# Alignment distances handed to the wavefront in two parts, and context rows loaded in their own order

## The chip, the cores and the metric

The kernel runs on one core of a Trainium2 chip. The metric is the time of one launch in microseconds (us). Five engines take part, each with its own instruction stream: TensorE (PE) for matmuls and transposes, VectorE (DVE), ScalarE (ACT), GpSimd (POOL), and SyncE (SP), which issues most DMAs. ACT and POOL issue DMAs as well. They meet only through semaphores: an instruction `wait_ge` stops the whole stream of the engine on which it stands.

## The reference, cut to what matters

Four blocks follow each other on `x` of 4 batches x 512 tokens x 128 channels, with a context of 4 x 77 keys x 128 channels. Only the first one is touched by the change:

```python
x = x + tanh(g_xattn[0]) * align(ctx_1024, layernorm(x))     # changed block
x = x + tanh(g_ffn[0])   * moe_64_experts(layernorm(x))
x = x + tanh(g_xattn[1]) * attention(layernorm(x), ctx_1024)
x = x + tanh(g_ffn[1])   * moe_8_experts(layernorm(x))

def align(small, large):                  # 77 keys, 512 tokens, per batch
    D = sqrt(max(aa[:, None] + bb[None] - 2 * small @ large.T, 0))
    R[i, j] = D[i, j] + min(R[i-1, j], R[i, j-1], R[i-1, j-1])
    walk back from (76, 511) to (0, 0) along the smallest neighbour
    expanded[j] += small[i]  for every cell (i, j) of that path
```

## The kernel before, in words

**Distances.** The recurrence over 77 x 512 cells is run from both ends at once: direction d = 0 takes the upper keys 0 to 38 (`HALF` = 39 rows, on partitions 0 to 38), direction d = 1 the lower keys in reverse order (`LOWER` = 38 rows, on partitions 64 to 101) with the tokens reversed too. `ctx_sb` holds the context in this order. The upper half is loaded by SP; the lower half is first copied row by row in reverse order into a scratch in device memory (`scr_ctx`, issued by ACT), then loaded from there by ACT. PE transposes `ctx_sb` (line 1056), ACT writes `ctxT_neg` and `ctxT` (lines 806, 809), DVE makes the squared sums `aa` (`context()`, lines 1508 and 1510). For each batch, the token rows are normalised on DVE and POOL, transposed on PE (`turn`), squared on ACT, and multiplied with `ctxT_neg` (`distances`, lines 1089 to 1093). ACT takes the root (`dist_root`, lines 840 to 844, with `aa` as the bias), DVE corrects it (`corrected`, lines 1522 to 1528) and counts `s_dist` up, once per batch.

**Lanes.** The recurrence runs as a wavefront. Tokens are cut into 15 chunks of 35 columns; chunk c of batch b is one partition (a lane), and at step s lane c handles row s - c. So a row of `d2` on one partition has to be spread over 15 partitions, each one slot later. This goes through the scratch `scr_d`: `store_dist` (line 457) writes 39 rows x 15 chunks of 140 bytes, `load_lanes` (line 464) reads 15 lanes of 53 slots (`SLOTS`) into `dl`. There are 8 stores and 8 loads (4 batches x 2 directions), all on SP but two loads that ACT issues. `scr_d` is zeroed beforehand (line 551, counted by `s_zero`).

**Forward steps.** DVE waits for all eight loads (`lanes_laid`) and then does 53 steps (lines 1571 to 1582). From step 38 on, each step has cells at which the two directions meet.

**Beside it.** PE, ACT, SP and POOL prepare 25 groups of second-MoE weights: SP loads a group (`load_prep`, lines 495 and 499, two buffers; the load of group g waits until PE has transposed group g - 2), PE transposes it (line 1131), ACT copies it (line 926), POOL stores it. On SP's queue the loads of groups 2 and up stand behind the last `load_lanes`. PE does parts of the value projection (lines 1109, 1110) after each of the first 12 groups, and the products that find the meeting column (`meet(c)`, lines 1117 and 1119) after groups 9, 10, 11 and 12, four per group (three after the last). DVE's `meeting()` (line 1610) waits for all fifteen.

**Backward steps.** 53 steps on DVE (lines 1628 to 1632) with the path cells made in pieces of four slots (`cells`, line 1605). Path cells go back to a row layout through `scr_on`, in three parts (`ON_PARTS` = slots 25 to 52, 5 to 24, 0 to 4): `store_path` (line 474) waits for the pieces of that part, and `load_path` (line 483, four DMAs, one per batch) for the store. SP does this for d = 0, ACT for d = 1. When all rows are there, PE makes the aligned sum (line 1153), and the next block begins.

Of the kernel before, what the change touches and what calls it, by code (L numbers as in the profile page):

```python
# [21 lines left out]
F32 = mybir.dt.float32  # L22
# [7 lines left out]
P = 128  # L30
# [6 lines left out]
def program(nc, x, ctx_1024, g_xattn, g_ffn, r0_w, sg0, su0, sd0, eg0, eu0, ed0,  # L37
# [14 lines left out]
    COLS = CH * CW  # L52
# [3 lines left out]
    DROWS = [slice(0, HALF), slice(64, 64 + HALF)]  # L56
    KROWS = 64 + HALF
# [3 lines left out]
    LSLOT = 64 + SLOTS  # L61
    LANE = LSLOT * CW
    ON_LANE = SLOTS * CW
    assert 2 * HALF - KEYS in (0, 1) and HALF <= 64 and 16 * B == 64
# [55 lines left out]
    with ctx:  # L120
# [13 lines left out]
        scr_ctx = nc.dram_tensor("scr_ctx", (B, LOWER, H), F32).ap()  # L134
# [29 lines left out]
        aa = sb("aa", [KROWS, B])  # L164
        aasq = sb("aasq", [KROWS, B, H])
# [6 lines left out]
        lane_table = sb("lane_table", [P, TABLE])  # L172
# [91 lines left out]
        ON_PARTS = [(25, SLOTS), (5, 25), (0, 5)]  # L264
# [94 lines left out]
        s_crev = sem("ctx_reversed")  # L359
# [30 lines left out]
        s_dst = [sem(f"dist_stored{b}") for b in range(B)]  # L390
        s_dld = sem("dist_lanes")
        s_upper = sem("wave_upper")
# [61 lines left out]
        def store_dist(engine, d, b):  # L454

            first = DROWS[d].start
            engine.dma_start(at(scr_d[b], first * CW, [[CW, HALF], [LANE + CW, CH], [1, CW]]),
                             d2[DROWS[d], b, :].rearrange("i (c w) -> i c w", w=CW)).then_inc(s_dst[b], 16)

        def load_lanes(engine, d, b):  # L460

            engine.wait_ge(s_dst[b], 32)
            first = FIRST_SLOT[d]
            engine.dma_start(dl[lanes(d, b)].rearrange("c s w -> c (s w)"),
                             scr_d[b, :, first:first + SLOTS].rearrange("c s w -> c (s w)")).then_inc(s_dld, 16)
# [4 lines left out]
        def store_path(engine, part, d):  # L470

            first, last = ON_PARTS[part]
            engine.wait_ge(s_on, 2 * ON_PIECES[part])
            engine.dma_start(scr_on[d, :, :, first:last, :].rearrange("b c s w -> (b c) (s w)"),
                             on[64 * d:64 * (d + 1), first:last].rearrange("c s w -> c (s w)")).then_inc(s_onst[d], 16)

        def load_path(engine, part, d):

            first, last = ON_PARTS[part][0], (HALF, LOWER)[d] if part == 0 else ON_PARTS[part][1]
            engine.wait_ge(s_onst[d], 16 * (part + 1))  # L480
            for b in range(B):
                cells = pmask[64 * d + first:64 * d + last, b, PAD * (1 - d):PAD * (1 - d) + COLS].rearrange("i (c w) -> i c w", w=CW)
                engine.dma_start(cells if d == 0 else cells[:, ::-1, :],
                                 at(scr_on[d, b], first * CW,
                                    [[CW, last - first], [ON_LANE + CW, CH], [1, CW]])).then_inc(s_path[d], 16)
# [20 lines left out]
        POOL_CONST = 25  # L506
# [143 lines left out]
        def _(pool):  # L650
            for p0 in (32, 96):
                nc.gpsimd.memset(ctx_sb[p0:p0 + 32], 0.0).then_inc(s_cz, 1)
            pool.wait_ge(s_cz, 2)
# [47 lines left out]
            pool.wait_ge(s_pool, 20)  # L701
            lane_constants(slice(0, 16), 0, 0)
            pool.wait_ge(s_pool, 24)
# [98 lines left out]
        def _(act):  # L802
            def context():
                act.wait_ge(s_ct, 1)
                turned = ps[6].rearrange("p (b r) -> p b r", b=B)
                nc.scalar.activation(ctxT_neg[:], turned, ACT.Copy, scale=-2.0).then_inc(s_ctn, 1)
                for first, rows in ((0, slice(0, HALF)), (HALF, slice(64, 64 + LOWER))):
                    n = rows.stop - rows.start
                    nc.scalar.activation(ctxT[:, :, first:first + n], turned[:, :, rows], ACT.Copy).then_inc(s_ctn, 1)

            def lane_tables():

                act.wait_ge(s_lt, 1)
                nc.scalar.activation(lane_table[:], ps[7][:, 0:TABLE], ACT.Copy).then_inc(s_lc, 1)
                nc.scalar.activation(rst[:, 0, 0:1], ps[7][:, CORNER:CORNER + 1], ACT.Copy).then_inc(s_lane, 1)
# [21 lines left out]
            def dist_root(b):  # L837

                act.wait_ge(s_ab, b + 1)
                nc.scalar.activation(d2[0:KROWS, b, 0:S], dist_bank(b)[0:KROWS], ACT.Relu, bias=aa[:, b:b + 1]).then_inc(s_d2, 1)  # L840
# [11 lines left out]
            def norm(k):  # L852
                for b in range(B):
                    root(k, b)
                    if k == 0 and b == 0:
                        context()
                    if b >= 1:
                        high(k, b - 1)
                    if k == 0 and b == 1:
                        lane_tables()  # L860
                    if k == 2 and b >= 2:
                        query(b - 2)
                if k == 0:
                    act.wait_ge(s_aa, 1)
# [11 lines left out]
            act.wait_ge(s_cz, 2)  # L876
            act.wait_ge(s_crev, 16)
            act.dma_start(ctx_sb[64:64 + LOWER], scr_ctx.rearrange("b k d -> k b d")).then_inc(s_ctx, 16)
# [13 lines left out]
            for b in (2, 3):  # L892
                load_lanes(act, 1, b)
# [28 lines left out]
            for g in range(GROUPS[1]):  # L922
# [129 lines left out]
        def _(pe):  # L1052
# [5 lines left out]
            pe.wait_ge(s_pool, 24)  # L1058
            nc.tensor.matmul(ps[7][:, 0:TABLE], repeat_lane[:], by_lane[:], start=True, stop=True).then_inc(s_lt, 1)

            def turn(k, b):
# [10 lines left out]
                mm.then_inc(s_xt, 1)  # L1072

# [8 lines left out]
            def distances(b):  # L1082
# [5 lines left out]
                top, bottom = dist_bank(b)[0:64, :], dist_bank(b)[DROWS[1], :]  # L1088
                nc.tensor.matmul(top, ctxT_neg[:, b, 0:64], xT0[:, b, :], start=True, stop=False)
                nc.tensor.matmul(bottom, ctxT_neg[:, b, DROWS[1]], xT0[:, b, ::-1], start=True, stop=False)  # L1090
                pe.wait_ge(s_sq, b + 1)
                nc.tensor.matmul(top, ones[:, 0:64], sq[:, b % 2, :], start=False, stop=True)
                nc.tensor.matmul(bottom, ones[:, 0:HALF], sq[:, b % 2, ::-1], start=False, stop=True).then_inc(s_ab, 1)
# [292 lines left out]
        def _(dve):  # L1386
# [118 lines left out]
            def context():  # L1505

                dve.wait_ge(s_ctx, 32)
                sq_step = done(nc.vector.tensor_tensor(aasq[:], ctx_sb[0:KROWS], ctx_sb[0:KROWS], ALU.mult))
                after(sq_step)
                nc.vector.tensor_reduce(aa[:], aasq[:], AX_X, ALU.add).then_inc(s_aa, 1)  # L1510
# [3 lines left out]

            norm(0, loaded)
# [47 lines left out]
            for s in range(SLOTS):  # L1563
# [34 lines left out]
            def cells(g):  # L1598
# [336 lines left out]
```

## Time and profile before

| | |
|---|---|
| median of 3 runs | 776.57 us (772.94 to 778.0) |
| the profiled execution's own time | 773.22 us |
| its span, from first to last instruction | 771.5 us |
| busy in the span: PE, DVE, ACT, POOL | 85%, 74%, 51%, 46% |
| mean granted TensorE clock | 0.895 |

The times of rows are us from the start of the span. The changed block is the stretch from 0 to some 137 us; from there to the end the other three blocks follow.

### The profile page before, as it was taken

Reading aid. Unit: us, or ns where it says so; the run is one execution under the profiler, and the core shown is the slowest. Engines: PE = TensorE matmul, PEld = TensorE weight load, DVE = VectorE, ACT = ScalarE, POOL = GpSimd, SP = SyncE. Lnnn points to the kernel's source line nnn. Section 1 sums busy time; section 2 is a strip of 40 time slices with the busy share of each in tenths; the row PEclk is TensorE's granted clock in tenths of the full one; section 3 lists DMA queues with packets and bytes.
Section 4 is the critical chain, followed back from the end, with each engine's and each line's share of the span. In section 5 each row is a group of like instructions: output and inputs, shape, how many; then the busy total and the mean of one; then the engine's idle time right before and its main releaser. Section 6 shows DMA issues by size and latency. Waiting matters only on the chain.

```text
span 771.5 us, 13248 instructions
## 1 busy us (share of the span) xinstructions
PE 658.5 (85%) x3526; PEld 502.0 (65%) x3526; DVE 572.8 (74%) x1631; ACT 396.1 (51%) x705; POOL 354.1 (46%) x328
## 2 busy tenths in 40 slices
PE   4447520689999999999999959988989999999996
PEld 1134310577878788888888736655768888877885
DVE  6559995777777777777777685789867777777775
ACT  3642220345556555655655544455445655655554
POOL 5011120355666666666666560000256666666664
PEclk9755555689999999999999977999799999999999
DMA  5563553038767867776776300000157756666661
GB/s 137 86 127 115 149 157 59 3 74 179 155 129 156 158 138 148 154 148 135 162 150 137 75 2 1 3 2 12 38 96 155 159 140 145 158 148 133 157 152 55
DMA packets 82713, 86.55 MB, mean 112 GB/s; under 512 B 40642, under 2 KB 61651, under 8 KB 79731
## 3 DMA queue, kind: packets, MB, share of 16 engines
q1 hardware_dynamic: 78073, 80.01, 48.9%
q0 software_dynamic: 1600, 4.92, 1.7%
q10 hardware_dynamic: 3002, 1.17, 0.8%
q8 instruction: 17, 0.28, 0.2%
q14 instruction: 21, 0.17, 0.1%
HBM read 76.92 MB, written 9.23 MB: 112 GB/s over the span
## 4 chain that ended last, share of the span: by engine, by line
PE 69%; DVE 17%; issue 4%; DMA 4%; ACT 2%; POOL 1%; ACTq 1%; SPq 0%; DVEq 0%; POOLq 0%
PE bank L1159 7%; PE bank L1161 7%; PE bank L1160 7%; PE bank_quad L1315 7%; PE bank_pair L1161 7%; PE bank_pair L1159 7%; PE bank_pair L1160 7%; PE bank_quad L1312 7%; PE bank_quad L1313 7%; DVE arena L1632 2%; DMA scr_d<-arena 2%; PE bank_pair L1208 2%; PE bank L1251 2%; DVE rden L1762 1%; DVE arena L1628 1%
## 5 line engine op out<-in xcount | busy, mean ns | idle before, releaser
L779 POOL TENSOR_TENSOR act_lo<-arena,act_hi 128x512 fp32r<-128x512 f32 x232 | 300.3, 1295 | 193.0 <-ACT act_hi L966 191.8
L980 ACT ACTIVATE arena<-bank 128x512 f32<-128x512 f32 x232 | 138.7, 598 | 185.7 <-PE bank L1161 185.6
L1866 DVE TENSOR_TENSOR bank_pair<-arena,bank_pair 128x512 f32<-128x512 f32 x220 | 152.4, 693 | 103.1 <-ACT arena L980 72.4
L1874 DVE TENSOR_TENSOR arena<-bank_pair,arena 128x512 f32<-128x512 f32 x220 | 152.1, 691 | 16.9 <-DMA arena<-scr_mask 4.7
L966 ACT ACTIVATE act_hi<-arena 128x512 fp32r<-128x512 f32 x232 | 144.6, 623 | 13.4 <-DVE arena L1864 7.4
L1315 PE MATMUL bank_quad<-act_lo,w_hi 128*128 128x512 f32 x232 | 92.7, 400 | 3.8 <-POOL act_lo L779 3.8
L1159 PE MATMUL bank_pair<-xn_hi,w_hi 128*128 128x512 f32 x232 | 93.1, 401 | 2.7 <-DVE arena L1864 1.5
L1159 PE MATMUL bank<-xn_hi,w_hi 128*128 128x512 f32 x232 | 93.5, 403 | 0.0
L1161 PE MATMUL bank<-xn_lo,w_hi 128*128 128x512 f32 x232 | 92.9, 400 | 0.0
L1160 PE MATMUL bank<-xn_hi,w_lo 128*128 128x512 f32 x232 | 92.6, 399 | 0.0
L1161 PE MATMUL bank_pair<-xn_lo,w_hi 128*128 128x512 f32 x232 | 92.6, 399 | 0.0
L1160 PE MATMUL bank_pair<-xn_hi,w_lo 128*128 128x512 f32 x232 | 92.6, 399 | 0.0
L1312 PE MATMUL bank_quad<-act_hi,w_hi 128*128 128x512 f32 x232 | 92.2, 398 | 0.0
L1313 PE MATMUL bank_quad<-act_hi,w_lo 128*128 128x512 f32 x232 | 92.0, 396 | 0.0
L714 POOL TENSOR_SCALAR xn<-x_res,mv,rstd 128x128 f32<-128x128 f32 x16 | 14.0, 878 | 131.9 <-DVE rstd L1422 81.4
L1315 PEld LDWEIGHTS bank_quad<-act_lo,w_hi 128*128 128x128 f32 x232 | 43.7, 188 | 17.3 <-POOL act_lo L779 6.9
L1159 PEld LDWEIGHTS bank_pair<-xn_hi,w_hi 128*128 128x128 f32 x232 | 44.2, 191 | 14.3 <-DVE arena L1864 2.0
L1850 DVE TENSOR_TENSOR w_lo<-w_raw,w_hi 128x384 fp32r<-128x384 f32 x54 | 51.7, 958 | 0.1
L1159 PEld LDWEIGHTS bank<-xn_hi,w_hi 128*128 128x128 f32 x232 | 44.3, 191 | 11.6 <-issue 1.8
L1160 PEld LDWEIGHTS bank_pair<-xn_hi,w_lo 128*128 128x128 f32 x232 | 44.2, 191 | 10.8
L1161 PEld LDWEIGHTS bank_pair<-xn_lo,w_hi 128*128 128x128 f32 x232 | 44.1, 190 | 10.9
L1161 PEld LDWEIGHTS bank<-xn_lo,w_hi 128*128 128x128 f32 x232 | 44.1, 190 | 10.8
(248 smaller groups left out, 965.4 us busy)
## 6 DMA issues: line engine op xcount, KB each, us to landing
arena<-scr_mask SPq DMA_DIRECT2D x94, 512.0 KB, 6.3
scr_w<-prep_out POOLq DMA_DIRECT2D x25, 192.0 KB, 2.6
w_raw<-scr_w SPq DMA_DIRECT2D x25, 192.0 KB, 6.5
w_raw<-in_L_ffn_expert_gate_k SPq DMA_DIRECT2D x32, 64.0 KB, 5.9
w_raw<-in_L_ffn_expert_up_k SPq DMA_DIRECT2D x32, 64.0 KB, 5.6
w_raw<-in_L_ffn_expert_down_k SPq DMA_DIRECT2D x64, 32.0 KB, 5.2
prep_in<-in_L_ffn_wg SPq DMA_DIRECT2D x21, 64.0 KB, 1.9
prep_in<-in_L_ffn_wu SPq DMA_DIRECT2D x21, 64.0 KB, 2.0
```

Source lines behind the costliest of these rows:

```text
L779: nc.gpsimd.tensor_tensor(act_lo[:, k % 2, :], act_a[:, k % 2, :], act_hi[:, k % 2, :].bitcast(F32), ALU.subtract).then_inc(FF[f]["alo"], 1)
L966: nc.scalar.activation(act_hi[:, j, :], act_a[:, j, :], ACT.Copy).then_inc(FF[f]["ahi"], 1)
L980: nc.scalar.activation(act_s[:, k % 2, :], ps[4 + k % 2][:], ACT.Silu).then_inc(FF[f]["silu"], 1)
L1159: nc.tensor.matmul(out, w_h, x_h, start=start, stop=False)
L1160: nc.tensor.matmul(out, w_l, x_h, start=False, stop=False)
L1161: return nc.tensor.matmul(out, w_h, x_l, start=False, stop=stop)
L1312: nc.tensor.matmul(ps[n][:], w_hi[:, j, DOWN:DOWN + P], act_hi[:, i, :], start=first, stop=False)
L1313: nc.tensor.matmul(ps[n][:], w_lo[:, j, DOWN:DOWN + P], act_hi[:, i, :], start=False, stop=False)
L1315: nc.tensor.matmul(ps[n][:], w_hi[:, j, DOWN:DOWN + P], act_lo[:, i, :], start=False, stop=last).then_inc(FF[f]["down"], 1)
L1850: nc.vector.tensor_tensor(w_lo[:, j, :], w_raw[:, j, :], w_hi[:, j, :].bitcast(F32), ALU.subtract).then_inc(FF[f]["wlo"], 1)
L1866: nc.vector.tensor_tensor(ps[6 + i][:], act_s[:, i, :], ps[6 + i][:], ALU.mult).then_inc(FF[f]["t"], 1)
L1874: nc.vector.tensor_tensor(act_a[:, i, :], ps[6 + i][:], mask[:, j, 512 * k:512 * (k + 1)], ALU.mult).then_inc(FF[f]["act"], 1)
```

## The change

Four edits. (1) The lower half of the context is loaded as it stands, both halves by ACT straight after one DVE fill of `ctx_sb`; ACT reads the transposed columns backwards when it writes `ctxT_neg`, and the squared sums, now in natural order, are brought into the order of the distances by one product with a constant `flip` matrix, made on POOL. (2) `store_dist` and `load_lanes` take a range of rows or slots: rows 0 to 15 and slots 0 to 15 first, then the rest (24 rows, since a half now has 40 rows, and 37 slots), the rest of d = 0 on SP and of d = 1 on ACT. DVE waits for the rest only at step 16. (3) The lane-table product moves on PE behind the first transposes of the tokens, together with the `flip` product. (4) The path cells of d = 1 are laid out reversed, because `ctx_sb` is no longer reversed, and the last two path parts are cut at slot 13 instead of 5.

```diff
-    DROWS = [slice(0, HALF), slice(64, 64 + HALF)]
-    KROWS = 64 + HALF
+    FIRST_ROWS, DIST_ROWS = 16, 40
+    KROWS = 64 + DIST_ROWS
-        ON_PARTS = [(25, SLOTS), (5, 25), (0, 5)]
+        ON_PARTS = [(25, SLOTS), (13, 25), (0, 13)]
...
+        def later_rows(engine, d):
+            engine.wait_ge(s_zero, 16 * -(-LSLOT // SLOTS))
+            engine.wait_ge(s_dist, B)
+            for b in range(B):
+                store_dist(engine, d, b, FIRST_ROWS, DIST_ROWS, s_dst2[d])
+        def later_lanes(engine, d):
+            for b in range(B):
+                engine.wait_ge(s_dst[b], 32)
+            engine.wait_ge(s_dst2[d], 16 * B)
+            for b in range(B):
+                load_lanes(engine, d, b, FIRST_ROWS, SLOTS, s_dld2)
...
 # SP
-                if b == 0:
-                    sp.wait_ge(s_cz, 2)
-                    sp.dma_start(ctx_sb[0:HALF], ctx_1024[:, 0:HALF].rearrange("b k d -> k b d")).then_inc(s_ctx, 16)
...
                 for d in range(2):
-                    store_dist(sp, d, b)
-                if b in (1, 2):
+                    store_dist(sp, d, b, 0, FIRST_ROWS, s_dst[b])
+                if b >= 1:
+                    sp.wait_ge(s_dst[b - 1], 32)
                     for d in range(2):
-                        load_lanes(sp, d, b - 1)
-            for b in (2, 3):
-                load_lanes(sp, 0, b)
+                        load_lanes(sp, d, b - 1, 0, FIRST_ROWS, s_dld)
+            sp.wait_ge(s_dst[B - 1], 32)
+            for d in range(2):
+                load_lanes(sp, d, B - 1, 0, FIRST_ROWS, s_dld)
+            later_rows(sp, 0)
+            later_lanes(sp, 0)
             for g in range(2, GROUPS[1]):
                 load_prep(sp, g, *prep_span(g))
...
 # POOL
-            for p0 in (32, 96):
-                nc.gpsimd.memset(ctx_sb[p0:p0 + 32], 0.0).then_inc(s_cz, 1)
+            for first, step in ((0, -1), (64, 1)):
+                nc.gpsimd.affine_select(out=flip[:, first:first + 64], in_=ones[:, 0:64], compare_op=ALU.is_equal, fill=0.0,
+                                        base=first - MIRROR if first else 0, pattern=[[step, 64]], channel_multiplier=1).then_inc(s_pool, 1)
...
 # ACT
-                nc.scalar.activation(ctxT_neg[:], turned, ACT.Copy, scale=-2.0).then_inc(s_ctn, 1)
+                nc.scalar.activation(ctxT_neg[:, :, 0:64], turned[:, :, 0:64], ACT.Copy, scale=-2.0)
+                nc.scalar.activation(ctxT_neg[:, :, 64:KROWS], turned[:, :, MIRROR - KROWS + 1:MIRROR - 64 + 1][:, :, ::-1],
+                                     ACT.Copy, scale=-2.0).then_inc(s_ctn, 1)
...
-            act.dma_start(scr_ctx, at(ctx_1024, (KEYS - 1) * H, [[KEYS * H, B], [-H, LOWER], [1, H]])).then_inc(s_crev, 16)
+            act.wait_ge(s_cz, 1)
+            for first, keys in ((0, slice(0, HALF)), (64, slice(HALF, KEYS))):
+                act.dma_start(ctx_sb[first:first + keys.stop - keys.start], ctx_1024[:, keys].rearrange("b k d -> k b d")).then_inc(s_ctx, 16)
...
-            act.wait_ge(s_crev, 16)
-            act.dma_start(ctx_sb[64:64 + LOWER], scr_ctx.rearrange("b k d -> k b d")).then_inc(s_ctx, 16)
...
-            for b in (2, 3):
-                load_lanes(act, 1, b)
+            later_rows(act, 1)
...
                 nc.scalar.activation(prep_out[:, g % 2, :], ps[7][:, 0:WIDE], ACT.Copy).then_inc(s_pout, 1)
+                if g == 0:
+                    later_lanes(act, 1)
...
 # PE, after the transposes of the first batch
+                pe.wait_ge(s_pool, 26)
+                nc.tensor.matmul(ps[7][:, 0:TABLE], repeat_lane[:], by_lane[:], start=True, stop=True)
+                pe.wait_ge(s_aa, 1)
+                nc.tensor.matmul(ps[7][:, TABLE:TABLE + B], flip[:], aa[:], start=True, stop=True).then_inc(s_lt, 1)
...
 # DVE
+            nc.vector.memset(ctx_sb[:], 0.0).then_inc(s_cz, 1)
             norm(0, loaded)
...
+                if s == FIRST_ROWS:
+                    dve.wait_ge(s_dld2, 16 * 2 * B)
...
-                    out_half = on[half, s0:s1, :] if d == 0 else on[half, s0:s1, ::-1]
+                    out_half = on[half, s0:s1, :] if d == 0 else on[half, SLOTS - s1:SLOTS - s0, :][:, ::-1, ::-1]
```

## Rows read from the trace of the kernel before

**Rows 1.** The chain that ended last, 0 to 160 us: start, duration, what.
```profile
4.45 5.49 DMA ctx_sb<-scr_ctx
...
43.92 3.75 DMA arena<-scr_d
48.16 0.23 DVE arena L1579
...
56.85 0.22 DVE arena L1579
...
136.71 2.06 PE bank L1153 x8
```

**Rows 2.** Timeline, 0 to 25 us: start, duration, engine, line, what [idle before <-releaser].
```profile
9.96 0.69 DVE L1508 TENSOR_TENSOR aasq<-ctx_sb 103x512 f32<-103x512 f32 x1 [1.76 <-DMA ctx_sb<-scr_ctx]
...
11.14 0.60 ACT L806 ACTIVATE ctxT_neg<-bank_pair 128x512 f32<-128x512 f32 x1 [5.43 <-PE bank_pair L1056]
...
12.30 0.18 DVE L1464 RECIPROCAL rstd<-std 128x4 f32<-128x4 f32 x1 [0.93 <-ACT std L821]
```

**Rows 3.** Landing times of the token loads, view of tile x_res.
```profile
DMA to landing us min/median/max: 2.7/3.7/4.7
```

**Rows 4.** Timeline, 24.5 to 48.5 us.
```profile
25.22 3.56 SPq L457 DMA_DIRECT2D scr_d<-arena  x4
...
31.01 0.77 SPq L464 DMA_DIRECT2D arena<-scr_d  x2
...
31.83 0.88 SPq L457 DMA_DIRECT2D scr_d<-arena  x2
32.03 0.83 DVE L1528 TENSOR_TENSOR arena<-arena 103x512 f32<-103x512 f32 x1
...
36.15 0.88 SPq L457 DMA_DIRECT2D scr_d<-arena  x2
40.92 3.32 SPq L464 DMA_DIRECT2D arena<-scr_d  x2
...
44.29 0.37 SPq L495 DMA_DIRECT2D prep_in<-in_L_ffn_swg  x1
...
47.77 0.01 DVE L1571 LOAD_MASK_SELECT arena<-arena  x1 [13.96 <-DMA arena<-scr_d]
```

**Rows 5.** Timeline of PE, 44 to 112 us.
```profile
48.73 0.90 PE L1131 MATMUL bank_pair<-ident,prep_in 128*128 128x128 f32 x3 [0.87 <-DMA prep_in<-in_L_ffn_wd]
...
51.59 0.87 PE L1131 MATMUL bank_pair<-ident,prep_in 128*128 128x128 f32 x3 [0.81 <-ACT prep_out L926]
...
68.72 0.66 PE L1110 MATMUL bank_quad<-bv_row,ones 1*52 1x128 f32 x2
72.14 0.28 PE L1117 MATMUL bank_quad<-arena,meet_pick 128*4 128x35 f32 x2 [2.76 <-DVE arena L1579]
...
77.57 0.90 PE L1131 MATMUL bank_pair<-ident,prep_in 128*128 128x128 f32 x3
...
80.62 0.90 PE L1131 MATMUL bank_pair<-ident,prep_in 128*128 128x128 f32 x3
```

**Rows 6.** Timeline of SP, 44 to 112 us.
```profile
53.71 2.45 SPq L499 DMA_DIRECT2D prep_in<-in_L_ffn_wd  x2
```

**Rows 7.** Timeline of DVE, 70 to 86 us.
```profile
82.26 0.69 DVE L1610 MAX8 meet_top<-bank_quad 4x8 f32<-4x512 f32 x1 [0.16 <-PE bank_quad L1119]
```

**Rows 8.** Timeline of ACT, 44 to 135 us.
```profile
115.05 3.40 ACTq L483 DMA_DIRECT2D arena<-scr_on  x4
```

**Rows 9.** Timeline, 118 to 139 us.
```profile
125.19 0.70 DVE L1605 TENSOR_TENSOR arena<-arena 64x175 f32<-64x175 f16 x2
...
126.77 3.12 ACTq L483 DMA_DIRECT2D arena<-scr_on  x4
...
131.90 3.05 ACTq L483 DMA_DIRECT2D arena<-scr_on  x4
```

**Rows 10.** Landing times of all path stores, view of tile scr_on.
```profile
DMA to landing us min/median/max: 2.0/2.8/3.1
```

More of the change, by code:

```diff
@@ L60, in program @@
     FIRST_SLOT = [0, 64]
-    LSLOT = 64 + SLOTS
+    LSLOT = 64 + SLOTS + 1
+    MIRROR = 2 * 64 + LOWER - 1
     LANE = LSLOT * CW
     ON_LANE = SLOTS * CW
-    assert 2 * HALF - KEYS in (0, 1) and HALF <= 64 and 16 * B == 64
+    assert 2 * HALF - KEYS in (0, 1) and HALF <= DIST_ROWS and 16 * B == 64
     def lanes(d, b):
@@ L163, in program @@
         iota_e = sb("iota_e", [P, E1])
-        aa = sb("aa", [KROWS, B])
-        aasq = sb("aasq", [KROWS, B, H])
+        aa = sb("aa", [P, B])
+        aasq = sb("aasq", [P, B, H])
+        flip = sb("flip", [P, P])
         TABLE = 2 + 2 * CH
@@ L390, in program @@
         s_dst = [sem(f"dist_stored{b}") for b in range(B)]
+        s_dst2 = [sem(f"dist_later_stored{d}") for d in range(2)]
         s_dld = sem("dist_lanes")
+        s_dld2 = sem("dist_later_lanes")
         s_upper = sem("wave_upper")
@@ L452, in prep_rows, with store_dist, load_lanes @@
             return found
[L454 to L465, printed above, removed]
+        def store_dist(engine, d, b, first, last, stored):
+            rows = slice(64 * d + first, 64 * d + last)
+            engine.dma_start(at(scr_d[b], rows.start * CW, [[CW, last - first], [LANE + CW, CH], [1, CW]]),
+                             d2[rows, b, :].rearrange("i (c w) -> i c w", w=CW)).then_inc(stored, 16)
+        def load_lanes(engine, d, b, first, last, loaded):
+            engine.dma_start(dl[lanes(d, b), first:last].rearrange("c s w -> c (s w)"),
+                             scr_d[b, :, FIRST_SLOT[d] + first:FIRST_SLOT[d] + last].rearrange("c s w -> c (s w)")).then_inc(loaded, 16)
+        def later_rows(engine, d):
[9 more added lines that the diff above has]
+                load_lanes(engine, d, b, FIRST_ROWS, SLOTS, s_dld2)
         def lanes_laid(engine):
@@ L473, in store_path @@
             engine.wait_ge(s_on, 2 * ON_PIECES[part])
+            if d == 1:
+                first, last = SLOTS - last, SLOTS - first
             engine.dma_start(scr_on[d, :, :, first:last, :].rearrange("b c s w -> (b c) (s w)"),
@@ L480, in load_path @@
             engine.wait_ge(s_onst[d], 16 * (part + 1))
+            at_slot, lane_step = (first, 1) if d == 0 else (SLOTS - last, -1)
+            row = first if d == 0 else 64 + LOWER - last
             for b in range(B):
-                cells = pmask[64 * d + first:64 * d + last, b, PAD * (1 - d):PAD * (1 - d) + COLS].rearrange("i (c w) -> i c w", w=CW)
+                cells = pmask[row:row + last - first, b, PAD * (1 - d):PAD * (1 - d) + COLS].rearrange("i (c w) -> i c w", w=CW)
                 engine.dma_start(cells if d == 0 else cells[:, ::-1, :],
-                                 at(scr_on[d, b], first * CW,
-                                    [[CW, last - first], [ON_LANE + CW, CH], [1, CW]])).then_inc(s_path[d], 16)
+                                 at(scr_on[d, b], at_slot * CW,
+                                    [[CW, last - first], [ON_LANE + lane_step * CW, CH], [1, CW]])).then_inc(s_path[d], 16)
         def load_prep(engine, g, r0, r1):
@@ L505, in program @@
         block = ctx.enter_context(nc.Block())
-        POOL_CONST = 25
+        POOL_CONST = 27
         @block.sync
@@ L700, in _ @@
             lane_constants(slice(0, 32), 16, 17)
-            pool.wait_ge(s_pool, 20)
+            pool.wait_ge(s_pool, 22)
             lane_constants(slice(0, 16), 0, 0)
-            pool.wait_ge(s_pool, 24)
+            pool.wait_ge(s_pool, 26)
             def attention_prep():
@@ L813, in lane_tables @@
                 act.wait_ge(s_lt, 1)
-                nc.scalar.activation(lane_table[:], ps[7][:, 0:TABLE], ACT.Copy).then_inc(s_lc, 1)
+                nc.scalar.activation(lane_table[:], ps[7][:, 0:TABLE + B], ACT.Copy).then_inc(s_lc, 1)
                 nc.scalar.activation(rst[:, 0, 0:1], ps[7][:, CORNER:CORNER + 1], ACT.Copy).then_inc(s_lane, 1)
@@ L839, in dist_root @@
                 act.wait_ge(s_ab, b + 1)
-                nc.scalar.activation(d2[0:KROWS, b, 0:S], dist_bank(b)[0:KROWS], ACT.Relu, bias=aa[:, b:b + 1]).then_inc(s_d2, 1)
+                nc.scalar.activation(d2[0:KROWS, b, 0:S], dist_bank(b)[0:KROWS], ACT.Relu,
+                                     bias=lane_table[0:KROWS, TABLE + b:TABLE + b + 1]).then_inc(s_d2, 1)
                 act.wait_ge(s_d2, b + 1)
@@ L863, in norm @@
                 if k == 0:
-                    act.wait_ge(s_aa, 1)
+                    act.wait_ge(s_lc, 1)
                     dist_root(0)
@@ L1057, in _, with tables @@
             mm.then_inc(s_ct, 1)
-            pe.wait_ge(s_pool, 24)
-            nc.tensor.matmul(ps[7][:, 0:TABLE], repeat_lane[:], by_lane[:], start=True, stop=True).then_inc(s_lt, 1)
+            def tables():
+                pe.wait_ge(s_pool, 26)
+                nc.tensor.matmul(ps[7][:, 0:TABLE], repeat_lane[:], by_lane[:], start=True, stop=True)
+                pe.wait_ge(s_aa, 1)
+                nc.tensor.matmul(ps[7][:, TABLE:TABLE + B], flip[:], aa[:], start=True, stop=True).then_inc(s_lt, 1)
             def turn(k, b):
@@ L1072, in turn @@
                 mm.then_inc(s_xt, 1)
+                if k == 0 and b == 0:
+                    tables()
             def norm(k, after=None):
@@ L1507, in context @@
                 dve.wait_ge(s_ctx, 32)
-                sq_step = done(nc.vector.tensor_tensor(aasq[:], ctx_sb[0:KROWS], ctx_sb[0:KROWS], ALU.mult))
+                sq_step = done(nc.vector.tensor_tensor(aasq[:], ctx_sb[:], ctx_sb[:], ALU.mult))
                 after(sq_step)
```

12 lines of the change are left out of this document (4 added, 8 removed).

## The prediction

> **What bounds the kernel now.** I read the page's busy shares first: PE 85%, DVE 74%. The change touches none of the expert stages in which PE is busy throughout, so I went through the chain of waits from 0 to 160 us [rows 1], then each engine's timeline. The touched block is three waits and two long DVE runs. First, until 9.94 everything waits for the lower context rows (4.45 + 5.49). Second, distances are ready at 32.86, yet DVE starts its steps only at 47.77, after 13.96 us idle [rows 4]: the stores and loads of the lanes. Third, the last path cell is made at 125.89 [rows 9] and the aligned sum starts at 136.71 [rows 1]. Between them lie 53 forward steps, 0.621 us each at first ((56.85 - 48.16) / 14 [rows 1]), then the meeting, then 53 backward steps.
>
> What decides is a second chain beside the forward steps. DVE waits 0.16 us for PE at the meeting, at 82.26 [rows 7], and PE's last meeting product ends at about 82.2. PE had waited only 2.76 us in front of its first one, at 72.14 [rows 5]. So the weight groups, whose loads stand on SP's queue behind the lane loads, run nearly level with the forward steps. That cover is 2.76 us thick: a DVE that starts earlier gets there before PE.
>
> **Context.** Removed: the round trip through scratch. The last context DMA is now issued at about 1.8, after a fill of 128 x 512. Its landing: between the 2.7 us of the fastest token load [rows 3] and the 5.49 of the load with the same bytes [rows 1]. I take 6.0, because the same shape is the nearest row and three token loads of 256 KB now stand around it: 7.8 instead of 9.94. From the landing to DVE's reciprocal, before: 12.30 - 9.96 = 2.34 (PE's transposes, then ACT) [rows 2]. ACT's first copy becomes two, more by 0 to 0.60 [rows 2], taken as 0.1, since the columns in sum get fewer. So 7.8 + 2.4 = 10.2 instead of 12.3. DVE's own limit: it is free at 9.96 - 1.76 = 8.20 and `context()` takes (12.30 - 0.93) - 9.96 = 1.41, so 9.6 [rows 2]. Gain 2.1, ends 0 and 2.7. On PE the lane-table and flip products now stand between the transposes of the first and second batch; PE has room until the second batch is normalised, which comes after `context()`. The two POOL selects stand where POOL only waits. I take 2.0: distances ready at 30.9 instead of 32.86.
>
> Row and rule agree on the slow landing, and the rule tells what the change leaves alone. The Trainium skill, page "DMA: Bandwidth & Descriptors", section "Why a DMA increments its semaphore by 16 and not by 1", says that a hardware-queued DMA uses as many engines, at most 16, as divide the slowest dimension of both sides. For 38 rows that makes 2, for 39 rows 13, for 16 rows 16, for 24 rows 12. By it the lower context load stays a two-engine load; a price of 5.49 rather than 2.7 would follow.
>
> **First part of the lanes.** A pair of stores landed 5.8 us after its issue on a quiet queue (25.22 to 31.01) and 7.8 us later with loads in between (36.15 to 43.92, where the load that waits for it is issued) [rows 4]. The new pairs have 16 of 39 rows. SP now waits for the pair of batch b - 1 right behind the store of batch b, and what is queued behind is the next store: pair 1 is issued at about 26.0 (28.0 before, the third and fourth of the four issues from 25.22 on [rows 4]), has landed at 31 at a price of 5, two loads take 0.77, so pair 3 goes at 31.9 instead of 36.15. ACT's four later stores are issued at the same time. I take 6.3 us for pair 3 (ends 4 and 7.8): 38.2. Two loads (0.77) and a landing, 3.75 before [rows 1] for 53 slots, taken as 3.3 for 16: DVE starts at 42.3, 5.5 us earlier (ends 3 and 8).
>
> **Second part.** SP's four later stores start at 39.0. They carry 96 rows against 78 of a pair; taken at the 7.8 us of the slower pair, they have landed at 46.8 (ends 45 and 50). Four loads at 0.36 (0.77 for two) follow, to 48.3. They land 3.75 later, at 52.0. DVE reaches step 16 at 42.3 + 16 x 0.621 = 52.2, so this wait costs nothing, and has 4 us more of slack at the meeting. ACT's own part waits for its own earlier stores and is over by then; behind it stand ACT's copies of weight groups, which no longer wait until 44.3 as before.
>
> **What the change triggers.** SP's loads of groups 2 and up move from 44.29 [rows 4] to 48.3, later by 4.0. Given back: group 3 waited for ACT's copy (0.81) [rows 5], which ACT now does earlier; and one SP issue of two DMAs took 2.45 [rows 6], where two issues elsewhere took 0.88 [rows 4], so 0 to 1.5 may vanish; together I take 1.3 (ends 0.8 and 2.3). PE is ready to meet at 68.72 + 0.66 = 69.4 before [rows 5]. From there, never waiting for DVE, it has 1.6 for the last group with three meetings (80.62 to 82.2, of which 0.9 is the transposes [rows 5]), so some 0.95 for four meetings, and 3.05 for each of the two groups between (80.62 - 77.57 [rows 5]): 0.95 + 6.1 + 1.6 = 8.65, to 78.0. After: 78.0 + 4.0 - 1.3 = 80.7. DVE's steps end at about 82.1 - 5.5 = 76.6, so PE binds, and the meeting gains 82.2 - 80.7 = 1.5, not 5.5. Ends: second part landed at 45 with 2.3 given back, 77.9 (gain 4.3); at 50 with 0.8, 84.4 (loss 2.2).
>
> **Path parts.** The last part grows from 5 slots to 13; the middle part is stored two pieces (8 backward steps, about 6 us) earlier. Before, ACT was still issuing the middle part's loads until 129.89, and only then could the last part be stored [rows 9]. Now the store goes at 125.9, lands within 2.0 to 3.1 [rows 10] (taken 2.6; 114 KB lie between the sizes that made these), ACT issues four loads in 3.05 and the last lands 1.76 later, as before (131.90 + 3.05 to 136.71) [rows 1, 9]: 133.3 instead of 136.7. Cover: ACT must be through with the middle part by then. Its first part ends at 118.45 [rows 8]; 3.1 for the middle store and 3.1 for its loads make 124.7, 1.2 us to spare. Gain 3.2 (ends 2.3 and 3.6). The doubly reversed cells on DVE have no row; 0 taken, ends -0.1 and +0.1 on each of 13.
>
> **Sum.** 1.5 + 3.2 = 4.7. The context's 2.0 and the lanes' are inside the 1.5. What follows 137 us shifts as a whole. The profiled execution took 773.22 (span 771.5 and 1.7 around it): 768.5. The median of the runs is 3.35 above it, 776.57, and they spread over 5 us; against the median 771.9.
>
> **Rivals.** (A) PE doesn't bind: the second part lands by 45, the slow issue goes away, and DVE's 5.5 us come through whole, with 3.2 of the path: 8.7, time 767.9. For: ACT's share of the stores no longer stands on SP's queue. Against: only 2.76 us of slack, against 4.0 of delay. (B) Slower: both queues' later stores and the first parts delay each other. A price for this is in the rows: with loads mixed in, the pair of batch 2 was issued at 31.83 and its load, which waits for it, at 40.92, 9.1 us [rows 4]. Pair 3 at 31.9 + 9.1 = 41.0, later stores from 41.8 at 9.1 x 96 / 78 = 11.2: 53.0. Loads of groups at 54.5, PE at 78.0 + 10.2 - 1.3 = 86.9, 4.7 late; minus 3.2, slower by 1.5: 778.1. It turns slower from a second part landed at 51.5 on, 1 us for each further one. (C) The front doesn't do what it says: the lower context lands near 10 all the same, and 2.0 are lost on every later time up to the meeting: gain 4.7 - 2.0 = 2.7, time 773.9.
>
> For B speaks the Trainium skill, "Trainium Kernel Development and Optimization", section "Key Constraints": DMAs from SP, ACT and POOL run on the same 16 engines, and more issuers save only issue time. No row before shows two such streams of stores together.
>
> **How the numbers follow.** Forecast 0.6, A 0.18, B 0.1, C 0.12. About 1% (7.8 us) is what a measurement of this kernel can tell from no change. Faster by more is A, and a little of the forecast's upper end: 0.2. Slower by more takes a loss of 7.8 + 3.2 at the meeting, so a second part landed at 59, where even B's 53 falls short: 0.04. Within 1%: 0.76. Range: the forecast's own ends are a loss of 2.2 with a gain of 2.3, and 4.3 with 3.6, so 776.5 and 768.7. A lies below that at 767.9 and B above at 778.1; taking in nearly all of A, to 767, and going part of the way to B, to 777.5, leaves out no more than 2 in 10.
>
> **What would show it.** In the changed profile: ctx_sb landed at 7 to 8.5; DVE's first step at 41 to 43.5, without a wait at step 16 over 1 us; SP's first load of group 2 at 47 to 50; DVE idle in front of line 1610's MAX8 for 3 to 5 us, released by PE; no idle of PE in front of its first meeting product; path sum 7.5 us after the last cell instead of 10.8. I am wrong if the second part lands far from 46.8, since every us of it is one of the end, or if PE's groups run at another pace behind it.

## The result, and the profile after

| | before | after |
|---|---|---|
| median | 775.4 us (772.94 to 778.0, 4 runs) | 765.86 us (764.94 to 766.58, 4 runs) |
| the profiled execution: time, span | 773.22, 771.5 | 764.94, 763.2 |
| mean granted TensorE clock | 0.895 | 0.895 |

The ratio is 0.9884, 95% interval 0.9859 to 0.9908: 9.5 us between the medians, where I forecast 4.7, and below my range. In a second comparison (e2 below) it is 0.9888. Between the two profiled executions it is 8.3 us.

I read the changed kernel from the front to the back, at the same places as before. First the context, in its timeline (start, duration, engine, line, what, idle before and its releaser), with the DMA's own row from the chain that ended last:

```profile
1.50 0.94 ACTq L897 DMA_DIRECT2D ctx_sb<-in_ctx  x2
...
8.92 0.69 DVE L1538 TENSOR_TENSOR aasq<-ctx_sb 128x512 f32<-128x512 f32 x1 [0.71 <-DMA ctx_sb<-in_ctx]
```

```profile
2.19 6.71 DMA ctx_sb<-in_ctx
```

It landed at 8.92 instead of 9.96 [rows 2]: 1.0 us gained, of which 0.4 is left when the distances are ready (below). The rest is lost on PE ahead of the third batch, most of it at that batch's transposes (before, then after):

```profile
18.87 0.65 PE L1071 MATMUL bank_quad<-ident,xn 128*128 128x128 f32 x4
```

```profile
18.07 1.10 PE L1099 MATMUL bank_quad<-ident,xn 128*128 128x128 f32 x4
```

PE starts them 0.8 us earlier, but they take 1.10 us instead of 0.65. The granted clock is 1.00 in this stretch of both profiles, so why they were slower isn't shown. SP's queue, with the loads of the second group behind the lanes, and DVE's first step:

```profile
33.75 6.03 SPq L464 DMA_DIRECT2D arena<-scr_d  x4
39.88 1.77 SPq L459 DMA_DIRECT2D scr_d<-arena  x4
47.96 1.66 SPq L464 DMA_DIRECT2D arena<-scr_d  x4
49.66 0.34 SPq L514 DMA_DIRECT2D prep_in<-in_L_ffn_swg  x1
```

```profile
31.67 0.83 DVE L1559 TENSOR_TENSOR arena<-arena 104x512 f32<-104x512 f32 x1
...
43.37 0.01 DVE L1604 LOAD_MASK_SELECT arena<-arena  x1 [9.93 <-DMA arena<-scr_d]
```

The distances are ready at 32.50 (31.67 + 0.83), against 32.86 [rows 4], yet the steps start 4.4 us earlier. SP's later loads are issued at 47.96, when its later stores have landed, and group 2 goes at 49.66 instead of 44.29 [rows 4]. What this does to PE and to the meeting (DVE's MAX8, its first instruction behind the last meeting product):

```profile
53.41 0.90 PE L1161 MATMUL bank_pair<-ident,prep_in 128*128 128x128 f32 x3 [14.94 <-DMA prep_in<-in_L_ffn_wd]
...
72.39 0.28 PE L1147 MATMUL bank_quad<-arena,meet_pick 128*4 128x35 f32 x2
```

```profile
81.17 0.69 DVE L1643 MAX8 meet_top<-bank_quad 4x8 f32<-4x512 f32 x1 [3.35 <-PE bank_quad L1149]
```

PE no longer waits in front of its first meeting product, and DVE waits 3.35 us for the last, instead of 0.16 [rows 7]. The meeting gains 1.1 us, not 4.4. Last the path parts, from ACT's timeline and the chain:

```profile
119.28 3.15 ACTq L502 DMA_DIRECT2D arena<-scr_on  x4
124.85 0.51 ACTq L491 DMA_DIRECT2D scr_on<-arena  x1
127.40 3.33 ACTq L502 DMA_DIRECT2D arena<-scr_on  x4
```

```profile
124.85 2.53 DMA scr_on<-arena
...
129.93 2.71 DMA arena<-scr_on
...
132.78 2.06 PE bank L1183 x8
```

ACT is through with the middle part (119.28 + 3.15) before the last cell is made, and the sum follows the last cell by 8.0 us instead of 10.8. So the aligned sum starts at 132.78 instead of 136.71 [rows 1]: 3.9 us of the 8.3. The other 4.4 lie behind it, in stages that no line of the diff touches. To see where, take the start of ACT's Silu, which runs once per unit of the expert loops (one expert with 512 tokens, nine matmuls of 128x512 on PE). Before, units 20 and 125:

```profile
202.43 0.60 ACT L980 ACTIVATE arena<-bank 128x512 f32<-128x512 f32 x1 [0.90 <-PE bank L1161]
...
422.98 0.60 ACT L980 ACTIVATE arena<-bank 128x512 f32<-128x512 f32 x1 [0.98 <-PE bank L1161]
```

After:

```profile
197.52 0.60 ACT L1003 ACTIVATE arena<-bank 128x512 f32<-128x512 f32 x1 [0.89 <-PE bank L1191]
...
416.80 0.60 ACT L1003 ACTIVATE arena<-bank 128x512 f32<-128x512 f32 x1 [0.97 <-PE bank L1191]
```

(422.98 - 202.43) / 105 = 2.100 us per unit before, (416.80 - 197.52) / 105 = 2.088 after. Over some 232 units that is 2.8 us. The windows of this stretch (us, busy time and count of PE, of PE's weight loads, DVE, ACT, POOL, then granted clock, DMA share, GB/s), before and then after, say that it isn't the clock and isn't a wait: the clock granted is 1.00 in both, the 2.4 GHz level, PE is busy throughout, and it gets through 954 matmuls instead of 948.

```profile
202.00:423.00 221.00, 221.00 (x948) 177.19 (x947) 166.52 (x237) 130.99 (x237) 136.28 (x106) 1.00 0.73 148
```

```profile
202.00:423.00 221.00, 221.00 (x954) 178.44 (x953) 168.16 (x239) 132.45 (x239) 137.02 (x107) 1.00 0.73 150
```

What is left, some 1.6 us, is for the most part (1.5) waits for the expert masks (`arena<-scr_mask`) in the first units of each expert stage, in DVE's timeline of before and then of after; they differ from one execution of a kernel to the next, as e1 shows.

```profile
181.62 0.69 DVE L1874 TENSOR_TENSOR arena<-bank_pair,arena 128x512 f32<-128x512 f32 x1 [1.58 <-DMA arena<-scr_mask]
...
571.67 0.69 DVE L1874 TENSOR_TENSOR arena<-bank_pair,arena 128x512 f32<-128x512 f32 x1 [3.14 <-DMA arena<-scr_mask]
```

```profile
176.55 0.69 DVE L1907 TENSOR_TENSOR arena<-bank_pair,arena 128x512 f32<-128x512 f32 x1 [0.52 <-DMA arena<-scr_mask]
...
564.87 0.69 DVE L1907 TENSOR_TENSOR arena<-bank_pair,arena 128x512 f32<-128x512 f32 x1 [2.70 <-DMA arena<-scr_mask]
```

### The profile page after: what moved, and what is told of

Same layout as the page of the kernel before. It is cut to its first block, busy times and chain, and to the rows that moved or that the text cites. A ratio compares the mean times of both kernels' runs of the same rounds, so it can differ in the third digit from the quotient of the medians.

```text
span 763.2 us, 13274 instructions
## 1 busy us (share of the span) xinstructions
PE 657.4 (86%) x3528; PEld 505.1 (66%) x3528; DVE 573.4 (75%) x1632; ACT 396.4 (52%) x706; POOL 354.0 (46%) x328
## 4 chain that ended last, share of the span: by engine, by line
PE 71%; DVE 15%; DMA 4%; issue 3%; ACT 2%; POOL 1%; SPq 1%; ACTq 0%; DVEq 0%; POOLq 0%
PE bank L1189 7%; PE bank L1190 7%; PE bank_quad L1345 7%; PE bank L1191 7%; PE bank_pair L1189 7%; PE bank_quad L1342 7%; PE bank_pair L1190 7%; PE bank_pair L1191 7%; PE bank_quad L1343 7%; DVE arena L1665 2%; PE bank_pair L1238 2%; PE bank L1281 2%; DMA scr_d<-arena 2%; DVE rden L1795 1%; DMA prep_in<-in_L_ffn_wd 1%
## 5 line engine op out<-in xcount | busy, mean ns | idle before, releaser
L734 POOL TENSOR_SCALAR xn<-x_res,mv,rstd 128x128 f32<-128x128 f32 x16 | 14.1, 880 | 129.3 <-DVE rstd L1452 81.4
L1161 PE MATMUL bank_pair<-ident,prep_in 128*128 128x128 f32 x75 | 22.1, 431 | 35.9 <-DMA prep_in<-in_L_ffn_wd 32.2
L1190 PEld LDWEIGHTS bank<-xn_hi,w_lo 128*128 128x128 f32 x232 | 44.3, 191 | 10.5
```

The source lines that it names most:

```text
L1190: nc.tensor.matmul(out, w_l, x_h, start=False, stop=False)
```

## The experiments

Theory 1: the expert loops run at a slower or faster pace by chance, from one launch or chip to the next. Theory 2: something in the changed kernel sets the pace. The paces below are those of the first and the second expert stage, each between two Silu starts as above (units 20 to 125, and 154 to 224). "Sum" is the start of the aligned sum.

**e1_before_again and e2_after_again**: the two kernels once more, without an edit.

> The kernel before, unchanged, for a second trace on the chip of this group. In the two traces at hand the aligned sum starts 3.9 us earlier with the change, but the span is 8.3 us shorter; of the 4.4 us behind the sum, 2.7 lie in a steady pace of the expert loops (2.100 against 2.088 us per unit of nine matmuls) and 1.4 in two waits of VectorE for masks. Theory 1 (chip or execution, not kernel): this trace has the pace of the changed kernel's trace of the same group, within 0.003 us. Theory 2 (the kernel sets it): this one keeps 2.100 and the changed one keeps 2.088 on the same chip.

> The changed kernel, timed against the one before on the same chip. Theory 1 (the work ahead of the aligned sum gives 4 us, the rest is the chip's pace): 3.5 to 5.5 us faster, ratio 0.993 to 0.9955. Theory 2 (the gain behind the sum belongs to the change too): 8 to 10 us faster, ratio 0.987 to 0.990.

Before: 778.98 us, pace 2.101 and 2.100, sum at 137.09. After: median 766.05 (764.72 to 768.28), ratio 0.9888 [0.9857, 0.9919], pace 2.088 and 2.087, sum at 131.66. The pace belongs to the kernel: theory 1 falls. What does vary is the kernel before by itself: its second execution took 5.8 us more than the first, 5.5 of it by longer mask waits in units 11 to 14.

**e3_tail_only**: the kernel before with the new path parts alone.

```diff
-        ON_PARTS = [(25, SLOTS), (5, 25), (0, 5)]
+        ON_PARTS = [(25, SLOTS), (13, 25), (0, 13)]
```

> The kernel before with nothing but the path parts cut at slot 13 instead of 5. By the prediction's term the aligned sum starts 3.2 us earlier (2.8 by the changed kernel's trace) and the meeting stays at 82.2; so 2.8 to 3.3 us faster, ratio 0.996. The rival: the parts gain nothing by themselves because ScalarE is not through with the middle part in time, under 1 us.

771.91 us, ratio 0.9956 [0.9935, 0.9977], sum at 133.46, pace 2.100 and 2.101. The cut by itself is worth 3.25 us at the sum, or 3.0 if counted from MAX8, which came 0.26 us earlier in this execution. It leaves the pace alone.

**e4_groups_first**: the changed kernel, with SP's loads of two weight groups ahead of the wait for the later lanes.

```diff
             later_rows(sp, 0)
+            for g in range(2, 4):
+                load_prep(sp, g, *prep_span(g))
             later_lanes(sp, 0)
-            for g in range(2, GROUPS[1]):
+            for g in range(4, GROUPS[1]):
```

> The changed kernel with the loads of weight groups 2 and 3 moved on SP's queue from behind the later lane loads to the place ahead of the wait for them. Theory (the weight groups' start sets when PE is through with the meeting, DVE waits 3.35 us for it): group 2 on PE at 45 to 47 instead of 53.4, DVE's wait at the meeting gone, meeting at 77.5 to 78.5 instead of 81.2, and 2.5 to 3.5 us faster than the changed kernel. Rival (the loads collide with the later stores and lanes): the later lanes land 2 us or more later, DVE waits at step 16, and under 1 us is left.

763.73 us (762.43 to 764.73), ratio 0.9853 [0.9823, 0.9882]. SP issues group 2 at 41.56 instead of 49.66, and the meeting waits for nothing (SP's timeline, then DVE's):

```profile
41.56 0.41 SPq L514 DMA_DIRECT2D prep_in<-in_L_ffn_swg  x1
```

```profile
77.89 0.69 DVE L1645 MAX8 meet_top<-bank_quad 4x8 f32<-4x512 f32 x1
```

The sum starts at 129.30, 3.5 us before that of the changed kernel's first profile and 2.4 before that of e2, which ran on the same chip; between the medians of these two lie 2.3 us. That PE's groups bound the meeting is shown: with them out of the way DVE's earlier start comes through.

**e5_gap528 and e6_gap16**: no instruction changed. The diff allocates a new buffer, `flip`, and four more columns of `lane_table`, both ahead of the weight buffers `w_raw`, `w_hi` and `w_lo` and of `act_hi` and `act_lo`, from which PE reads in the expert loops. Theory 3: the place of these sets the pace. The kernel before, with an unused piece there:

```diff
+        gap = sb("gap", [P, P + B])        # e5; in e6 [P, B]
...
         w_raw = sb("w_raw", [P, 2, WIDE])
```

> The kernel before with one unused tile of 528 bytes per partition declared ahead of the weight and activation buffers, which is what the change adds there (512 for flip, 16 for four more columns of lane_table); no instruction differs. Four traces so far: 2.100 us per expert unit in the kernel before (twice) and with only the path parts changed, 2.088 in the changed kernel (twice) and with the groups moved. Theory (the place of the buffers sets the pace): 2.088 here, and some 2.7 us off the time, ratio 0.9965. Rival (something in the changed instruction streams sets it): 2.100 and ratio 1.000.

> As the run before, with an unused tile of 16 bytes per partition instead of 528. If the pace hangs on where the buffers start within a short line of memory (528 is 16 more than a multiple of 64), 2.088 as with 528; if on the larger shift, 2.100.

e5: 770.85 us (769.87 to 772.1), ratio 0.9963 [0.9947, 0.998], pace 2.089 and 2.088, sum at 137.16. e6: 770.01 us in one run, pace 2.089 and 2.088. Theory 3 holds: 2.7 us come from an unused piece of memory.

**e7_aligned**: I guessed that the weights want a multiple of 64 bytes, and moved them in e4 by 24 more, which by my count of the sizes made it so.

> The changed kernel with weight groups 2 and 3 loaded ahead, and an unused tile of 24 bytes per partition in front of w_raw, so that w_raw, w_hi and w_lo start at a multiple of 64 bytes by my count of the tiles. If the start within a line matters, the pace changes again, either way between 2.06 and 2.11 us per unit, so up to 6 us faster or 5 slower than the same kernel without the tile (763.7 us); if it doesn't, 2.088 and the same time.

765.85 us, ratio 0.9904 [0.9885, 0.9922], pace 2.098 and 2.099: 2.1 us slower than e4 by the medians, which come from two chips, and some 3.9 by the ratios (0.9904 against 0.9853), at nearly the same sum (129.51). The count was wrong, as the addresses below show.

**e8_lanes_in_one**: the changed kernel with the distances and lanes of a batch again in one part.

> The changed kernel with the distances stored and the lanes loaded in one part again, two of the loads on ScalarE's queue as before the change; the context, flip product and path parts stay changed. Theory (PE's weight groups bind the meeting, so the 5 us by which VectorE starts earlier are lost): VectorE starts its steps near 46.8, the meeting comes at 80.8 to 81.6, as in the changed kernel, and the time is within 1 us of it. Rival (the split is what gives the gain at the front): meeting at 83 or later, 2 us or more slower than the changed kernel.

765.69 us, ratio 0.9893 [0.9875, 0.9912], first step at 44.95, MAX8 at 79.51 after 0.16 us idle, sum at 130.92. The split of edit (2) gains nothing here: DVE starts later, but SP's groups go out earlier, and the meeting is no later for it.

**e9 to e12**: the kernel before with unused pieces at other places, to see which buffers matter.

```diff
# e9: [P, 4] here and [P, 12] ahead of prep_in;  e12: [P, 8] here
+        gap = sb("gap", [P, 4])
         w_raw = sb("w_raw", [P, 2, WIDE])
...
# e10: [P, 4] here and [P, 12] ahead of kT
+        gap = sb("gap", [P, 4])
         act_hi = sb("act_hi", [P, 2, 512], F32R)
         act_lo = sb("act_lo", [P, 2, 512], F32R)
# e11: [P, 4] here
+        gap = sb("gap", [P, 4])
         kT = sb("kT", [P, B * KEYS])
```

> The kernel before, with 16 unused bytes per partition ahead of the three expert weight buffers (w_raw, w_hi, w_lo) and 48 behind them, so that these three start 16 bytes later within a stretch of 64 and every other buffer starts where it did within one. No instruction is changed. Theory W (the place of the weights sets the pace of the expert loops): 2.088 us per unit, as after the shift by 16 bytes of everything, and a time near 771. Theory A (the place of act_hi and act_lo does): 2.100, and a time near 774 to 778. Theory R (the buffers behind both, the arena with the masks and act_a among them): 2.100. If the effect is shared, a pace between.

> The kernel before, with 16 unused bytes ahead of act_hi and act_lo and 48 behind them, so that only these two start 16 bytes later within a stretch of 64. Theory W: 2.100 us per unit. Theory A: 2.088. Theory R: 2.100.

> The kernel before, with 16 unused bytes behind act_lo: the weights, act_hi and act_lo stay, the attention buffers and the arena (in it the masks, act_a, act_s) move by 16 bytes. Theory W and theory A: 2.100 us per unit. Theory R: 2.088.

> The kernel before, with 32 unused bytes ahead of w_raw, so that everything from there on starts 32 bytes later instead of 16. If the pace goes by the place within 32 bytes, nothing changes: 2.100 us per unit, time 774 to 778. If it goes by the place within 64, or if any shift away from the old place helps, 2.088 or another value. The aligned sum stays near 137 in all four kernels.

Paces: e9 2.088 and 2.081, e10 2.094 and 2.093, e11 2.101 and 2.101, e12 2.088 and 2.089. Times of one run each: 772.68, 777.39, 776.16, 773.45. The buffers behind `act_lo` don't matter by themselves (e11); moving the two act buffers too (e10) gives half of the effect, moving the weights as well (e9, e12) the whole.

**e13_old_place**: the changed kernel with 496 unused bytes ahead of `w_raw`. **e14_old_parts**: the changed kernel with the old path parts (e3's diff turned round). **e15_groups_first_w**: e4 with [P, 12] ahead of `act_hi` and [P, 4] behind `act_lo`.

> The changed kernel with 496 unused bytes per partition ahead of the weight buffers, so that they and all behind them stand 528 + 496 = 1024 bytes behind their places in the kernel before, at the same place within every stretch of 64 to 1024 bytes. If the place explains the share of the gain that lies behind the aligned sum, the pace goes back to 2.100 us per unit and the time to 766.0 + 2.7 = 768.7, ratio 0.991; the aligned sum stays at 132 +- 1. If something else in the changed kernel makes the loops faster, the pace stays at 2.088 and the time at 766.0.

> The changed kernel with the path parts of the kernel before (the last two cut at slot 5 instead of 13). My sum gives 3.2 us for the cut: time 766.0 + 3.2 = 769.2 and aligned sum near 135.9, 10.8 us behind the last cell. The cut done by itself on the kernel before gave 3.25 at the sum and 3.5 on the median. Rival: with the meeting now earlier ACT is free sooner and half of it is lost: 767.6. Pace 2.088 in either case.

> The kernel with groups 2 and 3 loaded ahead of the later lanes (763.7 us, pace 2.088), and 48 unused bytes ahead of act_hi and 16 behind act_lo, so that the weights stand as in the changed kernel and act_hi and act_lo as in the kernel before, within 64 bytes. The kernel before with the weights alone moved ran at 2.088 and, in the second expert stage, 2.080. If that holds here, 0.007 x 102 units = 0.7 us less: 763.0, ratio 0.984. If the 2.080 was chance, 763.7.

e13: 766.81 us, ratio 0.9865 [0.9845, 0.9885], pace 2.088 and 2.089, against what I expected of the place. e14: 769.99 us, ratio 0.9926 [0.9905, 0.9947], sum at 135.13: 3.2 us more than e13, which ran beside it. e15: 763.37 us, ratio 0.9839 [0.9814, 0.9864], the fastest pace of all, 2.077 and 2.077; its ratio and that of e4 overlap. ACT's queue in e14, against that of the changed kernel above:

```profile
121.80 0.53 ACTq L491 DMA_DIRECT2D scr_on<-arena  x1
124.90 3.12 ACTq L502 DMA_DIRECT2D arena<-scr_on  x4
128.05 0.53 ACTq L491 DMA_DIRECT2D scr_on<-arena  x1
```

The last store waits until 128.05 for the issues of the middle part's loads, as before the change. In the changed kernel it goes when the cells are there.

**e16 to e18**: since e13 had spoken against the place, a sharper test. e16 is the changed kernel with `flip` and `lane_table` allocated behind everything else and 128 unused bytes where `lane_table` was, so that each old buffer has its old address. e17 and e18 are the kernel before with 512 and 1024 unused bytes ahead of `w_raw`.

```diff
-        flip = sb("flip", [P, P])
...
-        lane_table = sb("lane_table", [P, TABLE + B])
+        gap = sb("gap", [P, TABLE])
...
         arena = sb("arena", [P, ARENA])
+        flip = sb("flip", [P, P])
+        lane_table = sb("lane_table", [P, TABLE + B])
```

> The changed kernel with its two new pieces (flip, and lane_table with its four added columns) allocated behind the arena instead of ahead of the weights, and 128 unused bytes where lane_table was: every buffer that the kernel before also has now starts at exactly its old address. If place accounts for the faster loops inside the changed kernel, by a rule that goes over more than 1024 bytes, the pace goes back to 2.100 us per unit and the time to 766.0 + 2.7 = 768.7. If the pace stays at 2.088 and the time at 766.0, place doesn't account for it there, and something else of the change does.

> The kernel before with 512 unused bytes ahead of w_raw. If the place within 512 bytes decides, the pace stays at 2.100 us per unit; if any other place than the old one is good, 2.088 or less.

> The kernel before with 1024 unused bytes ahead of w_raw: the same displacement of the weights as in the changed kernel with 496 unused bytes, which ran at 2.088. If place decides and only the distance to the old place counts, 2.088 here too; if the place within 1024 bytes decides, 2.100, and then something else than place makes the changed kernel's loops faster.

e16: 771.8 us (769.5 to 776.37), ratio 0.9949 [0.9932, 0.9966], pace 2.100 and 2.101. e17: 774.81 us, 2.100 and 2.102. e18: 778.7 us, 2.100 and 2.101. The windows of e16:

```profile
202.00:423.00 221.00, 221.00 (x949) 177.07 (x948) 166.64 (x237) 131.27 (x237) 136.16 (x106) 1.00 0.73 147
```

949 matmuls, and the sum starts 1.6 us before that of the kernel before (135.07), unit 225 1.2 us before. With the addresses put back nothing is gained behind the sum. This settles the place inside the changed kernel too. The time is 3.1 us above the 768.7 that I had expected; in the profile 2.3 of this lie ahead of the sum, where MAX8 came at 83.64, the latest of all kernels with the new front. No run says whether that is chance.

**What the addresses say.** The addresses in the built programs show that each piece is rounded up to a multiple of 32 bytes. So my sizes were not what moved: 16 bytes were 32, the change itself moves the weights by 544 and not 528, e13 puts them 1056 behind the old place and not 1024. By these addresses, within 64 bytes:

| kernels | weights, act_hi and act_lo start at | pace |
|---|---|---|
| before, e1, e3, e7, e11, e16, e17, e18 | 32, 0 | 2.098 to 2.102 |
| e10 | 32, 32 | 2.094, 2.093 |
| after, e2, e4, e5, e6, e8, e12, e13, e14 | 0, 32 | 2.087 to 2.089 |
| e9, e15 | 0, 32 | 2.088 and 2.081; 2.077, 2.077 |

e13 no longer speaks against the place, and e7 moved the weights from a good place to a bad one. Open stays why e9 and e15 are faster than the others of their kind (in both, and in no other with weights at 0, the act buffers start at 96 within 128 bytes), and what a pair 0, 0 would give: it wasn't tried, so no run moves the weights alone. Why the loop is slower from one place than from another isn't shown by any run. The traces only show how it is spread: between 210 and 410 us the mean distance from the start of one product to the next is 233 to 234 ns at every place of the unit before, and 227 to 236 ns after.

## Why the prediction was wrong

**The step that failed** is the sentence "What follows 137 us shifts as a whole." It did not: 4.4 of 8.3 us between the profiled executions came from behind the aligned sum. Some 2.8 are the pace, which e5, e6 and e16 tie to the addresses of weight and act buffers. I had read the diff for instructions, waits and queues, and taken new buffers for nothing. The remaining 1.6 are for the most part mask waits, and these vary from one execution to the next.

A second step failed beside it. I added 3.35 us, the distance of the profiled execution of before from its median, to the changed kernel as well; its own distance is 0.9. Of the 6.0 us between the forecast 771.9 and the measured 765.86, 3.6 lie between the profiled executions (4.4 gained behind the sum, which I had not forecast, less 0.8 that I had forecast too much ahead of it) and 2.4 are this offset. The place alone, 2.8 us, would have given 769.1, inside my range.

**The terms ahead of the sum** were right in kind and near in size: forecast 4.7, measured 3.9 between the two profiles. By experiment on medians, e14 against e13 gives the path parts 3.2 us, and e16, which is the change without the place, gives 4.0 us for everything else by its ratio (0.0051 x 776.6).

- Context: landed at 8.92, forecast 7.8. The load that landed last took 6.71, longer than the 5.49 of the lower rows' bytes before [rows 1]. Distances were ready 0.4 us earlier, not 2.0. So 1.6 of 2.0 were lost, nearly what rival C says, but only half by C's way, a late landing; the rest went on PE, as shown above. It cost little because PE was the bound.
- First lanes: DVE's first step at 43.37 (42.56 in e2), forecast 42.3.
- Second part: stores landed at 47.96, forecast 46.8 (8.1 us for 96 rows, forecast 7.8). No wait at step 16. Rival B's price of 11.2 us did not show on SP. It nearly did on ACT: its four stores, issued at 32.59 beside SP's last pair and the first lanes, had landed only at 42.64, where its loads go, 10.0 us later (ACT's timeline):

```profile
32.59 2.30 ACTq L459 DMA_DIRECT2D scr_d<-arena  x4
...
42.64 1.70 ACTq L464 DMA_DIRECT2D arena<-scr_d  x4
44.38 0.49 ACT L947 ACTIVATE prep_out<-bank_pair 128x384 f32<-128x384 f32 x1 [8.08 <-issue]
```

  So ACT's copies of weight groups did stand until 44.4, as before and against what I wrote; this ended before SP's loads of group 2 and cost nothing. The Trainium skill, "Trainium Kernel Development and Optimization", section "Key Constraints", lets one expect that a second issuer saves only issue time. These rows don't speak against the rule: ACT's stores, beside SP's, took 10.0 us, and SP's later ones, which overlapped with them for at most 2.8 us, took 8.1. What the overlap itself costs isn't measured by any run.
- PE binds at the meeting, ready at 81.17, forecast 80.7, with DVE idle 3.35 us: right, and e4 shows it by taking it away (77.89). SP issued group 2 5.4 us later than before (49.66 against 44.29), forecast 4.0; PE had it 4.7 later (53.41 against 48.73 [rows 5]) and was ready to meet 3.0 later (72.39 against 69.4), so 1.7 was given back, forecast 1.3. Rival A falls: it would have needed the loads of the groups to be in time.
- Meeting gain 1.1 us, forecast 1.5. Over executions the place of MAX8 varies: 82.0 to 85.3 in the eleven profiles of kernels with the old front, 80.1 to 83.6 in five with the new one, means 83.4 and 81.4. So the mean gain is rather 2.0, of which the profile used for the forecast, an early one at 82.26, hid a part.
- Path parts: forecast 3.2. Measured 2.84 between the profiles (counted from MAX8 to the sum), 3.25 in e3, 3.2 in e14. The cover held: ACT was through at 122.43, forecast 124.7.

I named two ways to be wrong, both in front of the meeting. The true one was not among them.

## What to carry to other kernels

A change that adds or removes a buffer moves all that are allocated after it; where a long matmul loop reads from them, compare its pace per unit before and after, and test with an unused piece of memory, before an unexplained gain or loss far from the edit is put down to the edit. A wait that a queue serves for one engine delays all that stands behind it: two groups of loads moved ahead of one wait (e4) were worth some 2.3 us, and the split that made the wait necessary gave nothing by itself (e8). And the offset of one profiled execution from its median is not a property that the changed kernel inherits.

## What the runs showed of the hardware

The same nine matmuls of 128x512 took 2.100 us (before, e16) or 2.088 us (after, e13), and 2.077 at best (e15), at a granted clock of 1.00 and with PE busy throughout, by where the weights and the act buffers start within 64 bytes; for 232 units that is 2.8 us, up to 5.3. Moving by 512 or 1024 bytes left the pace at 2.100 to 2.102 (e17, e18). Each buffer took a multiple of 32 bytes, so an unused piece of 16 bytes moved the rest by 32 (e6). Four stores on ACT issued beside stores and loads on SP landed 10.0 us after the first issue, four of the same size on SP later in 8.1.
